# The first projection of a recurrent layer in two parts of 32 steps

## The reference

```
x   [2, 1024, 512]                                   (batch, time, dim)
a = layernorm(x)
u = a @ W_in.T + b_in                                [2, 1024, 1024]
s_t = tanh(u_t + s_(t-1) * gamma + beta)             1024 steps, each channel by itself
y = s @ W_out.T + b_out                              [2, 1024, 512]
x1 = x + layernorm(y)
h = layernorm(x1)
f = silu(h @ fp8(gate_w) * gate_scale) * (h @ fp8(up_w) * up_scale)     [2, 1024, 1536]
out = x1 + layernorm(f @ fp8(down_w) * down_scale)
```

## Time and profile before

| | |
|---|---|
| three runs | 561.14, 561.21, 562.38 us (median 561.21) |
| profiled execution | 561.96 us, span 560.2 us |
| mean granted TensorE clock | 0.991 |
| busy: PE / DVE / ACT / POOL | 542.8 (97%) / 446.3 (80%) / 375.3 (67%) / 248.4 (44%) us |

### The profile page before, as it was taken

One profiled execution on the slowest core, in us unless ns is written; L12 is line 12 of the kernel. 1 busy time (PEld: TensorE's weight loads), 2 busy tenths in 40 slices (PEclk: granted clock), 3 DMA queues, 4 the chain that ended last, 5 costly groups with the idle time before them and its releaser, 6 DMA issues.

```text
span 560.2 us, 11947 instructions
## 1 busy us (share of the span) xinstructions
PE 542.8 (97%) x2960; PEld 459.6 (82%) x2960; DVE 446.3 (80%) x2606; ACT 375.3 (67%) x2315; POOL 248.4 (44%) x372
## 2 busy tenths in 40 slices
PE   8998989899999999999999999999999999999994
PEld 5856758789789888898888888988888797899993
DVE  3688999988797899877997898878987998875314
ACT  2687686855678776876687767876787677752322
POOL 1122456564756533752348234552343243535531
PEclk9999989899999999999999999999999999999998
DMA  8789499972014100210003000300002000200011
GB/s 282 225 265 235 108 218 181 252 122 57 19 40 152 58 2 1 76 59 2 1 2 113 20 1 2 114 2 2 2 1 77 1 2 1 77 2 2 0 39 37
DMA packets 25333, 39.92 MB, mean 71 GB/s; under 512 B 3760, under 2 KB 8496, under 8 KB 25264
## 3 DMA queue, kind: packets, MB, share of 16 engines
q1 hardware_dynamic: 19904, 30.24, 16.3%
q0 software_dynamic: 4608, 8.39, 9.1%
q10 hardware_dynamic: 752, 0.54, 0.3%
HBM read 26.57 MB, written 4.20 MB: 55 GB/s over the span
## 4 chain that ended last, share of the span: by engine, by line
PE 82%; DVE 13%; ACT 3%; issue 1%; POOLq 0%; DVEq 0%; POOL 0%
PE gate_up L1110 31%; PE wide L1066 18%; PE wide L1136 15%; PE wide L1035 13%; DVE recur L1215 4%; DVE peaks L1414 2%; DVE powers L1397 2%; ACT pairs L1536 1%; PE recur_second L961 1%; PE wide L997 1%; DVE rounders L1404 1%; PE wide L1086 1%; PE gate_up L1066 1%; DVE recur L1206 1%; DVE x_lo L1404 0%
## 5 line engine op out<-in xcount | busy, mean ns | idle before, releaser
L1529 ACT ACTIVATE pairs<-recur 128x8 f32<-128x8 f32 x768 | 137.1, 178 | 91.1 <-DVE recur L1206 90.9
L1206 DVE TENSOR_TENSOR_SCAN recur<-recur,pairs 128x16 f32<-128x16 f32 x768 | 150.8, 196 | 50.1 <-ACT pairs L1529 47.5
L1529 ACT ACTIVATE pairs<-recur_second 128x8 f32<-128x8 f32 x768 | 136.8, 178 | 0.0
L1206 DVE TENSOR_TENSOR_SCAN recur_second<-recur_second,pairs 128x16 f32<-128x16 f32 x768 | 132.9, 173 | 0.0
L1718 POOL TENSOR_TENSOR fused_lo<-fused,fused_hi 128x256 fp32r<-128x256 f32 x95 | 69.9, 738 | 132.3 <-ACT fused_hi L1580 132.3
L1066 PE MATMUL wide<-w_out_sb,pairs 128*128 128x512 f32 (+1 forms) x272 | 112.9, 562 | 0.1
L1035 PE MATMUL wide<-x_norm_t,w_in_sb 128*128 128x256 f32 x448 | 102.3, 384 | 2.2 <-ACT x_norm_t L1480 1.7
L1035 PEld LDWEIGHTS wide<-x_norm_t,w_in_sb 128*128 128x128 f32 x448 | 85.4, 192 | 15.5 <-ACT x_norm_t L1480 2.4
L1066 PEld LDWEIGHTS wide<-w_out_sb,pairs 128*128 128x128 f32 x272 | 75.2, 298 | 24.2 <-issue 0.2
L1564 ACT ACTIVATE gated<-gate_up,gate_scale_cols 128x128 f32<-128x128 f32 (+1 forms) x168 | 63.4, 379 | 28.9 <-PE gate_up L1110 28.5
L1136 PE MATMUL wide<-down_q,fused_hi 128*128 128x512 f32 x192 | 81.2, 423 | 0.3 <-POOL fused_lo L1718 0.2
(11 more groups left out here) (134 smaller groups left out, 801.3 us busy)
## 6 DMA issues: line engine op xcount, KB each, us to landing
x_res<-x SPq DMA_DIRECT2D x16, 256.0 KB, 3.2
x_in<-x SPq DMA_DIRECT2D x14, 256.0 KB, 4.5
out<-z SPq DMA_DIRECT2D x14, 256.0 KB, 2.5
x_norm_t<-x_t SPq DMA_DIRECT2D x5, 512.0 KB, 3.4
raw_own<-rounders POOLq DMA_DIRECT2D x9, 256.0 KB, 4.8
w_in_sb<-w_in_t SPq DMA_DIRECT2D x4, 512.0 KB, 6.6
w_out_sb<-w_out_t SPq DMA_DIRECT2D x8, 256.0 KB, 3.9
raw_own<-down_w SPq DMA_DIRECT2D x8, 256.0 KB, 4.0
```

What stands on the lines that cost most here:

```text
L1206: eng.tensor_tensor_scan(preact_of[b].rearrange("p c k -> p (c k)"), factors_of[b].rearrange("p c k -> p (c k)"), pairs[:, t % RING, colum ...
L1529: ins = eng.activation(pairs[:, t % RING + 1, columns, 0], preact_of[b][:, :, 1], ACT.Tanh)
```

## The change

- The first half of block 0's projection is computed in two parts. `project_early_u` computes steps 0 to 31 of all eight heads (columns 0 to 63 of the tile, `EARLY_COLS` = 64), `project_first_u` steps 32 to 63 (columns 64 to 127) into the other half of the same bank columns, after the early copies of that bank. The second half (two quads) follows as before.
- ACT copies the early part before step 0 (`copy_early_u`, eight copies of 64 columns) and the late part between steps (`late_u_copy`, eight copies, two per pair of heads, from steps 1.7, 3.4, 5.1 and 6.8 on by the plan). Step 0 waits for the early copies, step 32 for the late ones, step 64 as before.
- Tile 1's transposes move behind all early products (place 34 instead of 29) and their copies behind all early copies (45 instead of 32). The bias moves behind the normalisation of tile 1 (14 instead of 11, against 12 and 13).
- Three zero products instead of four.
- The plan's TensorE is free from step 6 instead of -4, and all due steps are new. With them the order of nearly all planned jobs may move.

```diff
--- before.py
+++ after.py
@@ -140,24 +140,24 @@
 ISSUE_STEPS, LOAD_STEPS, LOAD_LANDS = 1.0, 1.5, 7.0
 ADD_ISSUE_STEPS, SETTLE_ISSUE_STEPS, SUM_STEPS, SUM_LANDS = 2.2, 1.9, 3.0, 6.0
 
-ENGINE_FREE = {"tensor": -4.0, "vector": -18.0, "scalar": -1.5, "gpsimd": -20.0, "sync": -24.0, "dma": -9.5}
+ENGINE_FREE = {"tensor": 6.0, "vector": -18.0, "scalar": -1.5, "gpsimd": -20.0, "sync": -24.0, "dma": -9.5}
 LAG = 3
 DOWN_RANK, NEGATE_RANK, ISSUE_RANK, PEAK_RANK, FIRST_X1_RANK, FIRST_CHUNKS_RANK = 20.0, 0.0, -2.0, 150.0, -4.0, -3.0
 
 
 
-CHUNKS_FROM = [165.19999999999928, 291.5, 439.69999999999965, 654.500000000001, 678.5000000000011, 877.9000000000019, 909.700000000003, 1041.0999999999974]
-CHUNKS_PER_BLOCK = [8, 13, 13, 10, 11.5, 11.5, 12, 13]
-INPUTS_FROM = [-408.40000000000384, 54.100000000000136, 104.50000000000045, 278.7000000000002, 461.60000000000014, 617.2000000000011, 815.9000000000003, 910.7999999999987]
-ROWS_FROM = [69.99999999999994, 175.89999999999998, 202.4999999999999, 227.1000000000002, 389.40000000000066, 413.999999999999, 541.0999999999999, 531.5999999999985, 706.8999999999992, 679.5999999999999, 743.9999999999998, 773.8999999999983, 912.5000000000006, 849.8999999999997, 1060.1999999999985, 1002.8999999999996]
-ROWS_TURNED = [114.40000000000023, 177.99999999999991, 288.69999999999936, 243.3999999999994, 415.3000000000007, 402.8, 608.0000000000002, 611.9999999999997, 725.5999999999987, 679.1999999999991, 836.1999999999997, 870.8999999999999, 928.6999999999999, 858.2999999999976, 1009.7000000000021, 1052.0000000000018]
+CHUNKS_FROM = [187.3999999999993, 305.39999999999975, 454.9999999999997, 576.5000000000008, 693.7000000000019, 796.3000000000031, 951.6000000000038, 1010.0999999999972]
+CHUNKS_PER_BLOCK = [9.5, 13, 8, 10.5, 9.5, 12.5, 12.5, 7]
+INPUTS_FROM = [-511.30000000000393, 69.40000000000009, 76.20000000000022, 377.0999999999999, 517.2000000000003, 811.4000000000008, 765.6000000000009, 830.4999999999978]
+ROWS_FROM = [35.999999999999986, 21.299999999999883, 165.79999999999995, 286, 388.00000000000034, 383.19999999999914, 503.4999999999996, 523.2999999999992, 644.8999999999988, 679.0000000000007, 740.9999999999998, 787.4999999999984, 824.2000000000006, 853.4000000000002, 1205.3999999999971, 1034.6000000000001]
+ROWS_TURNED = [133.90000000000035, 181.19999999999993, 292.2999999999993, 293.1999999999996, 472.0000000000008, 398.50000000000057, 598.1000000000003, 610.599999999999, 738.8999999999988, 679.5999999999993, 762.2999999999998, 823.8999999999994, 985.8999999999994, 990.8999999999967, 1088.9000000000028, 1084.1999999999998]
 TENSOR_MARGIN = 1.0
 GATE_UP_PIECES = 24
 TENSOR_FIRST = 16
 X2 = -1.2
 X_BEHIND = 8.0
 PEAKS_FROM = 60.0
-WARM_PRODUCTS = 4
+WARM_PRODUCTS = 3
 W_OUT_FROM, W_OUT_EVERY = 8.0, 6.0
 
 
@@ -441,8 +441,11 @@
         w_out_landed += load(("w_out", j), [(W_OUT_FROM + W_OUT_EVERY * j, 0.0)])
     weights()
 
+    for m in range(KH // 2):
+        for jj in range(2):
+            side("scalar", ("late_u_copy", m, jj), [(1.7 * (m + 1), 0.0)], 0)
     for q in range(2):
-        tensor(("first_u", q), FIRST_U_STEPS, [(0.0, 0.0)], -10.0)
+        tensor(("first_u", q), FIRST_U_STEPS, [(0.0, 0.0)] + [(("late_u_copy", q, jj), 0.2) for jj in range(2)], -10.0)
         for jj in range(4):
             side("scalar", ("first_u_copy", q, jj), [(("first_u", q), BEHIND_TENSOR)], 0)
     norm_x(1, x_landed[1], -2)
@@ -497,8 +500,9 @@
 
 
 HEAD = -60.0
-FIRST = {"x_half": ((0, 1), (7, 8)), "x_whole": (2, 9), "x_norm": (5, 12), "bias": 11, "t1": (20, 29), "t1_copy": (22, 32),
-         "first_u": (26, 28, 30, 32), "first_u_copy": (31, 33, 35, 37)}
+FIRST = {"x_half": ((0, 1), (7, 8)), "x_whole": (2, 9), "x_norm": (5, 12), "bias": 14, "t1": (20, 34), "t1_copy": (22, 45),
+         "early_u": (26, 28, 30, 32), "early_u_copy": (31, 33, 35, 37), "first_u": (35, 36, 37, 38)}
+EARLY_STEPS = 32
 
 
 def recurrent_sandwich_kernel(nc, x, x_t, w_in_t, w_out_t, b_in, beta, gamma, b_out, gate_w, up_w, down_w,
@@ -697,6 +701,8 @@
         s_x_scaled = sem("s_x_scaled")
         s_u_psum = sem("s_u_psum")
         s_u_rows = sem("s_u_rows")
+        s_early_psum = sem("s_early_psum")
+        s_early_u = sem("s_early_u")
         s_first_u = sem("s_first_u")
         s_first_half = sem("s_first_half")
         s_last_column = sem("s_last_column")
@@ -732,6 +738,7 @@
             return slice(h * HALF, (h + 1) * HALF)
 
         SPLIT = TWO_CHAINS_FROM * T
+        EARLY_COLS = batch * EARLY_STEPS
 
         def row_slice(kind, n, b, h):
 
@@ -980,10 +987,10 @@
                                                 ident[:, :])
                         ins.then_inc(s_t1, 1)
 
-            def project_first_u():
+            def project_early_u():
 
                 for m in range(MS):
-                    yield HEAD + FIRST["first_u"][m]
+                    yield HEAD + FIRST["early_u"][m]
                     if m == 0:
                         eng.wait_ge(s_first_half, 1)
                     eng.wait_ge(s_w_in_in[m], 16)
@@ -994,8 +1001,21 @@
                         for k in range(KD):
                             if j == 0 and k == KD // 2:
                                 eng.wait_ge(s_x_norm_t, 1)
-                            ins = eng.matmul(first_u_bank(j),
-                                             w_in_sb[:, k, j * P:(j + 1) * P], x_norm_t[:, k, 0:P],
+                            ins = eng.matmul(first_u_bank(j)[:, 0:EARLY_COLS],
+                                             w_in_sb[:, k, j * P:(j + 1) * P], x_norm_t[:, k, 0:EARLY_COLS],
+                                             start=(k == 0), stop=(k == KD - 1))
+                    ins.then_inc(s_early_psum, 1)
+
+            def project_first_u():
+
+                for m in range(MS):
+                    yield HEAD + FIRST["first_u"][m]
+                    eng.wait_ge(s_early_u, m + 1)
+                    for jj in range(2):
+                        j = 2 * m + jj
+                        for k in range(KD):
+                            ins = eng.matmul(first_u_bank(j)[:, EARLY_COLS:P],
+                                             w_in_sb[:, k, j * P:(j + 1) * P], x_norm_t[:, k, EARLY_COLS:P],
                                              start=(k == 0), stop=(k == KD - 1))
                     ins.then_inc(s_u_psum, 1)
                 for quad in range(QUADS):
@@ -1159,7 +1179,7 @@
                     eng.matmul(bank, signed_ident[:, 1, :], rounders[rounder_of[i]], start=False, stop=True
                                ).then_inc(s_rounded, 1)
 
-            weave(warm_up(), transpose_x(), project_first_u(), project_u(), project_y(), transpose_x1(), gate_up_products(),
+            weave(warm_up(), transpose_x(), project_early_u(), project_first_u(), project_u(), project_y(), transpose_x1(), gate_up_products(),
                   down_products(), round_weights())
 
 
@@ -1191,7 +1211,11 @@
             def recurrence():
                 for t in range(NB * T):
                     yield t - 0.01
-                    if t < T and t % TH == 0:
+                    if t == 0:
+                        eng.wait_ge(s_early_u, MS)
+                    elif t == EARLY_STEPS:
+                        eng.wait_ge(s_first_u, MS)
+                    elif t < T and t % TH == 0:
                         eng.wait_ge(s_first_u, MS + QUADS * (t // TH))
                     elif t % T == 0:
                         eng.wait_ge(s_u_rows, MS * (t // T))
@@ -1457,7 +1481,7 @@
                 yield HEAD
                 eng.wait_ge(s_warm, 1)
                 eng.activation(warm[:, 0:1], warm[:, 1:2], ACT.Silu)
-                yield HEAD + FIRST["first_u_copy"][0] - 0.5
+                yield HEAD + FIRST["early_u_copy"][0] - 0.5
                 eng.wait_ge(s_bias, 1)
 
             def sign_identity():
@@ -1487,17 +1511,30 @@
                 parts = [(0, m, wide[m], 2) for m in range(MS)] + [(1, quad, wide[quad], 4) for quad in range(QUADS)]
                 for part, (g, m, bank, columns) in enumerate(parts):
                     for jj in range(columns):
-                        yield HEAD + FIRST["first_u_copy"][m] + jj if g == 0 else at["first_u_copy", m, jj]
+                        yield at["late_u_copy", m, jj] if g == 0 else at["first_u_copy", m, jj]
                         j = columns * m + jj
-                        if g == 0 and j == KH - 2:
-                            eng.wait_ge(s_last_column, 1)
-                        elif jj == 0 or g == 0 and j == KH - 1:
+                        if jj == 0:
                             eng.wait_ge(s_u_psum, part + 1)
+                        slots = slice(EARLY_STEPS, TH) if g == 0 else input_slots(g * TH)
                         ins = eng.activation(
-                            pairs_by_batch[:, input_slots(g * TH), :, j, 1].rearrange("p s b -> p (s b)"),
-                            first_u_bank(j) if g == 0 else bank[:, jj * P:(jj + 1) * P], ACT.Identity,
```

(18 more changed lines are left out.)

## The result

The changed kernel takes 565.59 us (median of 6 runs, 564.13 to 566.63) against 561.07 us of the kernel before in the same runs: ratio 1.0078, 95% interval 1.0062 to 1.0093. It is 4.5 us slower. The forecast of 562.0 missed by 3.6 us, inside its range; the time is that of the rival "the backlog passes through" (565.7).

A forecast was written before the change was run, and what follows sets the result against it. TensorE was taken to bound the kernel, with room only in the head. Rounding 6.0 us later less 5.2 filled gave +0.8, above the recurrence's floor of -0.2: span 561.0, time 562.0, range 557.7 to 566.6.

The forecast's parts named there:

- the backlog passes through: Rival, chance 0.29: TensorE's extra 6.0 us hold until y(0,1), only 1.5 filled; +4.5 us, 565.7.
- one product less: Kernel start: dropping one zero product moves the transposes from 8.09 to 6.76; first projection matmuls start at 8.0, not 9.15.
- a pass of 64 columns costs what one of 128 does: Split first projection: 0.1116 us per 64-column matmul, so each part costs 7.14 us and TensorE gains 7.14 us of work.
- half the columns, half the time: Rival, chance 0.14: weight loads overlap better, each part of the split projection costs 3.6 us; 557.8.
- the start: Recurrence's start: scan 0 at 15.8, first tanh 16.45 (1.35 earlier), stalls at late copies, tanh 9 at 23.35, rounding from 30.0.
- then the waits of the earlier trace take it up: Head up to y(0,1): TensorE's waits and lost clock, 5.9 us, absorb 5.2 of the 6.0 us delay, leaving +0.8.
- y(0,1) within 2 us of 84.7: Sign of the forecast being right; a y(0,1) start over 2.5 us later would decide for the backlog rival.
- r = +1.4: Recurrence ends 1.4 us later, between -1.35 and +2.5; with 1.6 us of room, r-1.6 = -0.2 is the floor.
- New due steps: Reordering of the same instructions by the new due steps: cost 0, between -3.8 and +4 us.
- The clock: Two falls of TensorE's clock behind waits in the head, 1.7 us lost each, counted as room for backlog.
- clock stays low: Rival, chance 0.10: TensorE's clock rises only during the early part of the projection; 1.7 us more, 563.7.
- I leave them: From y(0,1) to the first gate product: waits at 92.44 and 105.20 and second clock fall, 3.8 us, assumed unchanged.

The follow-up runs named there:

- e1: Kernel before with three zero products, bias behind tile 1, tile 1's transposes and copies later; no split, old due steps: 560.88 us, ratio 0.9985.
- e9: Kernel before with only three zero products and the bias behind tile 1; no split, old due steps: 561.23 us, ratio 0.9986 to the kernel before.
- e5: Kernel before plus 32 products of zeros (64 passes) on TensorE between the projection's second half and rounding: 567.08 us, ratio 1.0103.
- e2: e1 plus the five new lists of due steps, still no split: 563.42 us, ratio 1.0039 to the kernel before.
- e3: Changed kernel with the five old lists of due steps: 570.7 us, ratio 1.0159 to the kernel before.
- e7: Changed kernel with one of four k slices in the late part, 16 passes instead of 64 (wrong input): 561.8 us, ratio 1.0019 to the kernel before.
- e11: Kernel before with zero products in two TensorE waits, before x1's transposes and the first gate product: 561.51 us, ratio 0.9996.

## Why the prediction came out as it did

**Right: one product less.** Transposes at 6.76, as worked out. The first pass stood at 8.31, not 8.0, held 0.65 us by the weights; e1 and e9 put the edit's worth at 0.8 us by their ratios, with intervals that reach to no change.

**Right, and what decides: a pass of 64 columns costs what one of 128 does.** 0.112 us, against 0.056 by columns. The extra work was put at 7.14 and measured at 7.10 (late part, 15.92 to 23.02). The estimate of 13.7 us for the two parts by the Trainium skill ("TensorE: Matmul & The Clock Gate", section "LDWEIGHTS (loading the stationary operand)") stands beside a measured 7.17+7.10 = 14.3, so the trace agrees with its rule within 5%. The rival "half the columns, half the time" is dead by this row alone.

**Right: the start.** Scan 0 at 16.08 (forecast 15.8), first tanh 16.65 (16.45), three stalls of 0.81, 0.92 and 0.91 us at the late copies, tanh 9 at 23.43 (23.35), rounding from 30.21 (30.0).

**Wrong: "then the waits of the earlier trace rows take it up", 5.2 of the 6 us.** This is the step that failed. I read an idle stretch of TensorE as room. It would be room if the engine that ends the wait were independent of TensorE. Here it is ScalarE, which takes rounded banks and copies turned x in an order written out beforehand, with the tanhs in between. ScalarE waits for TensorE at the first take; a late TensorE makes ScalarE late and, through the tanhs, the recurrence; and at 78 to 84 us the two meet with the same distance as before. e5 shows it bare: 6.4 us of backlog, all four waits unchanged, +5.5 us. In the changed kernel the 6.2 us at the first rounding are still 5.3 at the first transpose of x1 (83.93 against 78.66): some 1 us was absorbed there, not 5.2, and none of it by these waits. They are 0.37 us longer together (1.89+2.42 against 1.47+2.47), and 1.24 us went in the rounding, 20.85 us where it was 22.09. The prediction read this stretch as 16 rounds without a pause, through which the 6.0 us pass whole; there are 15, and they had small pauses. I had the sentence in the rival ("ScalarE, which is itself pushed back") and gave it 0.29 against 0.35, because 6 us is more than any one of the waits. The size of a wait says nothing on that; who releases it does.

**Half right by accident: y(0,1) at 85.41.** I named "y(0,1) within 2 us of 84.7" as a sign that the backlog was absorbed and 2.5 us as the point that decides for the rival. It came 0.7 late, and the rival won all the same. The new due steps had moved 16 passes of u(2,0), 3.45 us, from ahead of it to behind it (the group at 94.30 and the one at 105.09 are 64 passes where the earlier trace rows has 48), so the work was still to come: the first gate product is 3.2 us late. A milestone tests a backlog only if the same work lies before it.

**r = +1.4: right at step 9, wrong at the end.** The recurrence was 1.15 us late at tanh 9, 2.9 at steps 64 and 128, 3.3 at step 200, 3.8 at the end. Most of the first 1.8 us of this growth is VectorE's wait of 1.52 for a weight piece. The room of 1.6 us at the end was read rightly, and r-1.6 = 2.2 is a floor; but the place where the recurrence set the time is 177.60, which the prediction didn't look at, and there the changed order left no such room.

**New due steps, put at 0 between -3.8 and +4.** e1 and e2 give +3.0 us without the split, e3 and the change -4.5 with it. The sum of the change is not a sum of parts. Of e3's extra 4.5 us I can name the places (y(0,1) at 90.7, waits of 2.43, 1.48, 1.39 and 1.84 us in the head), but which list makes them was not tried.

**The clock.** The first fall stands (0.87), the second does not appear. The rival "clock stays low" in the first passes did not happen: the early passes ran at the pace of the late ones. The price of the two falls was about twice too high in my reading (3.4 against about 1.5 us).

**"I leave them": wrong on the other side.** The 3.8 us behind y(0,1) were filled by the new order. From the first transpose of x1 to the first gate product it is 24.43 us in the changed kernel (83.93 to 108.36) and 26.54 before (78.66 to 105.20), and the fall of the clock that followed there, 1.7 us of work, doesn't appear. But most of this was lost again: from 112 to 180 us TensorE waits 2.1 us (0.28, 0.21, 0.47 and 1.15) where it waited none before, the last time for the recurrence. So the 2.0 us absorbed in the end are a balance: about 1 us before 84, nearly 4 more up to 112, and some 3 given back behind it.

What stays open: how much of the loss behind 112 us belongs to the order and how much to the late recurrence. e7, whose recurrence was early, has the same waits, and e2 lost time there without the split; no run separates the two.

## What to carry to other kernels

Before splitting a matmul along its streamed columns, compare the stream with the weight load: with 128x128 weights in float32 here, 64 columns cost what 128 cost, so the split doubled the engine's time for that work. Join the second part to a neighbour that reads the same weights (192 columns at 0.164 us) and the split is nearly free. And count a wait of the bottleneck engine as room only when its releaser does not wait for that engine in turn; in a static order on all engines, backlog shifts the whole schedule and the waits with it. Look for such places all along the kernel: here the wait that set the time stood at 177.60, far behind the edit.

## What the runs showed of the hardware

Per pass, in float32 with 128x128 weights at the high clock: 0.112 us for 64 columns, 0.112 for 128, 0.164 for 192, 0.22 for 256. ScalarE's copy with bias from PSUM takes 0.37 us for 64 columns and 0.48 for 128, so halving it saves a quarter. I had put 0.33 for 64. The falls of TensorE's clock behind waits of 1.5 to 2.5 us come in some executions of one program and not in others (mean clock 0.988 to 0.997 in 75 runs of the kernel before; no fall in the traces of e1 and e9, whose waits there are 2.5 to 2.6 and 1.5 us). In all 11 runs of e11, whose waits at these places were 0.8 and 0.7 us long, the mean clock was 0.995 or more.
